# A four-layer graph network on one core: the last layer's first step sums its prepared chunks in place, and the degree count splits nodes by 800

## The chip, the cores and the metric

The kernel runs on one core of one Trainium2 chip. The metric is the device time of one execution in microseconds, lower is better. Each number of the trace comes from one profiled execution of the kernel.

## The reference

100,000 nodes with 64 features, 50,000 directed edges sorted by destination (a node has half an edge on the average). Four residual layers, each on `relu(layernorm(x))`: L0 is two graph convolutions with degree norms, L1 adds edge features, L2 is eight steps of edge attention, and L3, the last layer, is what the change is about. Cut to it:

```python
h = jnp.maximum(_layernorm(x), 0.0)
src_norm, dst_norm = deg(src) ** -0.5, deg(dst) ** -0.5     # degrees at least 1
out = w[0] * h
for step in range(10):
    m = (h * src_norm[:, None])[src]
    h = segment_sum(m, dst, 100000) * dst_norm[:, None]
    out = out + w[step + 1] * h
x = x + out
```

## The kernel before, in words

**Seats.** Every edge has a seat: 128 partitions by 392 columns (`COLS`), handled in 28 chunks of 14 columns (`CH`). Edges of one destination lie side by side in a partition, or run over into the next partition. `X[:, j, :]` holds the row of a seat's destination. After the dense part a step only works on seats: it gathers the 64 values of each seat's source, multiplies by `snE` (source norm), sums along the columns where `cont` is 1 (the same destination goes on; `sums`, L1807), multiplies by `dnorm`, adds it with weight `wk` to `X` and stores the rows as the table of the next step. Odd steps read `tab_e` and write `alt_e`, even ones the other way. A node whose source has no in-edges need not be followed further, so the seats are sorted by class, and each step gathers only the first columns: the widths `WI` are 252 columns or fewer for step two, and shrink from there.

**Step one.** It reads the rows of all 392 columns. The last ten chunks (`K3` = 10, from column `EARLY` = 252 on; 18 = `SPLIT`) have sources without in-edges, so their values come from the dense rows, and GpSimd gathers them into ten tiles ahead of the layer (`dead_rows`, L215 and L747): four in `shared`, two in `xin`, then `rowsC`, `agg`, `rowsD` (with rows 67 wide) and `spare`. If step two were wider than 252 the kernel would gather all 28 in step one (`full`, `past`, `WP`). In `step_e(1, True)` (L2258) VectorE first loops over nine pairs of gathered chunks, and then runs `last_chunk` (L2231) on the ten prepared ones in turn: it copies the rows into `G` (`copy_predicated`, L2246), multiplies, sums, multiplies with `dnorm` (L2251), and adds to `X` (L2254). The running sum `carry` passes from chunk to chunk.

**Around it.** GpSimd runs one list of work (L776): `narrow_sweep` (L660: per chunk a copy of 14 columns of indices at L672, then 14 indirect gathers at L483, buffers G[0] and G[1] in turn), ten scatters of finished rows to `out` (`early_rows`, L767), `front_sums` (L682: it waits until all stores of sums have landed, and gathers `tcar` and `FR`, the sums that cross a partition), four more scatters, `front_rows` (L691: it waits for `f_ready` and scatters `FR`), and then waits for `step_done`. ACT issues the stores of `G` (L851). VectorE turns the carried sums through PE twice (`carry_in`, L1828), signals `f_ready`, computes the next indices (`next_seats`, L2033) and waits until the early and the front rows have landed. `early_copy` (L2225) copies one chunk of `X` into `rowsA` for GpSimd's scatters, in step one after the first prepared chunk. In steps two to ten VectorE's loop has 14 turns, of which those that the width doesn't need are passed over at the start:

```python
wide_to = dve.value_load(WI[0:1, ds(k, 1)], min_val=0, max_val=COLS)
dve.reg_mov(at_pair, 0)
with dve.Fori(0, NCH // 2) as i:
    with dve.If(i * (2 * CH) + wide_to > COLS - 2 * CH):
```

After step ten VectorE signals `final_ready` (L2308), and GpSimd scatters the 252 remaining columns and the front row to `out` (L789 to L794).

**The degree count**, at the kernel's start. The number of edges of a source node is counted with products of one-hot vectors: node = `LOB` x hi + lo, with `LOB` = 1024. For each of the 392 columns VectorE compares a ramp with hi (128 columns) and with lo (1024 columns, L1321), and PE adds the products into two banks (L1099). Beside it GpSimd scatters the seats of 392 columns into `seatmap` (L522). VectorE then does the first dense tiles, and waits at L1484 until `seatmap` is read back, before it can write `lookup`.

## Time and profile before

| | before |
|---|---|
| median of 3 runs | 9275.63 us (9274.99 to 9276.62) |
| the profiled execution | 9275.27 us |
| its span | 9273.6 us |
| GpSimd, VectorE, PE busy | 6297.6, 5268.7, 1598.9 us |
| first gather of the last layer's step one | at 7219.11 us |
| first gather of its step two | at 7718.13 us |
| first of the scatters after step ten | at 8940.20 us |

The span is the time from the first to the last instruction that the profiler saw; 1.7 us of the execution lie around it. In the trace's rows PE, DVE (VectorE), ACT, POOL (GpSimd) and SP are the engines, a "q" behind one is its sequencer, which issues DMAs, and L483 is line 483 of the kernel. The indirect gathers all have the line of their helper, L483, and the scatters L487, so they are told apart by their tiles. The idle time in square brackets is that of the engine just before the instruction, with what ended it; "issue" means that the engine waited for nothing that the profile shows.

### The profile page before, as it was taken

Reading aid. Unit: us, or ns where it says so; the run is one execution under the profiler, and the core shown is the slowest. Engines: PE = TensorE matmul, PEld = TensorE weight load, DVE = VectorE, ACT = ScalarE, POOL = GpSimd, SP = SyncE. Lnnn points to the kernel's source line nnn. Section 1 sums busy time; section 2 is a strip of 40 time slices with the busy share of each in tenths; the row PEclk is TensorE's granted clock in tenths of the full one; section 3 lists DMA queues with packets and bytes.
Section 4 is the critical chain, followed back from the end, with each engine's and each line's share of the span. In section 5 each row is a group of like instructions: output and inputs, shape, how many; then the busy total and the mean of one; then the engine's idle time right before and its main releaser. Section 6 shows DMA issues by size and latency. Waiting matters only on the chain.

```text
span 9273.6 us, 59946 instructions
## 1 busy us (share of the span) xinstructions
PE 1598.9 (17%) x7434; PEld 1131.8 (12%) x7434; DVE 5268.7 (57%) x16349; ACT 581.8 (6%) x1205; POOL 6297.6 (68%) x6351
## 2 busy tenths in 40 slices
PE   5635231310355203530012200000000000000000
PEld 1124221210244202320012100000000000000000
DVE  6668464673888853446678777555548454333310
ACT  0012110100122101110000000000001000000000
POOL 6767766547777777767767577676556755677777
PEclk9855555555555555555555555555555555555555
DMA  0023111110344423333333322133322221433220
GB/s 11 4 78 108 59 61 34 66 40 0 89 134 129 120 84 82 95 82 91 91 97 113 84 46 49 42 46 42 37 30 72 48 45 41 43 42 40 35 27 19
DMA packets 604655, 568.99 MB, mean 61 GB/s; under 512 B 437740, under 2 KB 443809, under 8 KB 604496
## 3 DMA queue, kind: packets, MB, share of 16 engines
q0 software_dynamic: 189536, 151.31, 12.7%
q10 hardware_dynamic: 368192, 328.20, 10.7%
q1 hardware_dynamic: 46866, 88.94, 2.9%
q14 instruction: 56, 0.46, 0.0%
q8 instruction: 5, 0.08, 0.0%
HBM read 214.35 MB, written 357.06 MB: 62 GB/s over the span
## 4 chain that ended last, share of the span: by engine, by line
POOL 46%; issue 23%; DVE 18%; DMA 10%; POOLq 1%; DVEq 1%; PE 0%; SPq 0%; ACTq 0%; ACT 0%
POOL G L483 22%; POOL look L483 6%; DVE G L1821 5%; POOL X L483 4%; POOL pair L483 4%; POOL seatmap L487 4%; POOL out L487 3%; POOL spare L483 2%; DMA G<-tab_d,idxs 1%; DVE G L1811 1%; DMA alt_d<-G 1%; DVE xm L1370 1%; DMA G<-alt_d,idxs 1%; DVE st L1345 1%; DVE G L2103 1%
## 5 line engine op out<-in xcount | busy, mean ns | idle before, releaser
L483 POOL DMA_INDIRECT G<-tab_d,idxs x616 | 652.0, 1058 | 223.3 <-issue 178.3
L483 POOL DMA_INDIRECT look<-flagtab,idxs x588 | 613.2, 1043 | 206.7 <-issue 170.2
L483 POOL DMA_INDIRECT G<-tab_e,idxs x504 | 533.5, 1059 | 183.2 <-issue 151.9
L483 POOL DMA_INDIRECT G<-alt_e,idxs x420 | 445.0, 1060 | 157.7 <-issue 127.8
L483 POOL DMA_INDIRECT X<-in_x,dst_gat x392 | 417.0, 1064 | 154.5 <-issue 124.6
L483 POOL DMA_INDIRECT G<-tab_c,idxs x392 | 419.9, 1071 | 141.0 <-issue 111.2
L483 POOL DMA_INDIRECT G<-tab_b,idxs x392 | 419.1, 1069 | 141.1 <-issue 112.6
L483 POOL DMA_INDIRECT pair<-lookup,idxs x392 | 412.7, 1053 | 139.9 <-issue 116.1
L483 POOL DMA_INDIRECT G<-alt_d,idxs x392 | 408.8, 1043 | 141.6 <-issue 113.4
L2244 DVE TENSOR_TENSOR G<-G,chn 128x896 f32<-128x896 f32 x66 | 72.3, 1096 | 757.1 <-DMA G<-tab_e,idxs 409.2
L483 POOL DMA_INDIRECT G<-tab_a,idxs x392 | 396.7, 1012 | 142.7 <-issue 113.7
L487 POOL DMA_INDIRECT seatmap<-vals,idxs x392 | 397.7, 1015 | 140.7 <-issue 116.5
L1063 PE MATMUL TR<-w4T,shared 128*128 128x64 f32 x2356 | 464.6, 387 | 147.5 <-ACT shared L838 147.5
L1063 PEld LDWEIGHTS TR<-w4T,shared 128*128 128x128 f32 x2356 | 451.4, 298 | 241.3 <-issue 241.3
L1345 DVE BATCH_NORM_STATS2 st<-xin 128x6 f32<-128x64 f32 x3136 | 419.3, 211 | 61.4 <-DVE rowsC L1361 17.1
L1080 PE MATMUL HP<-ident,tcar 128*64 128x128 f32 (+1 forms) x21 | 8.7, 415 | 2523.6 <-DVEq L1281 2513.0
L1073 PE MATMUL TR<-w1Te,hT 64*128 64x64 f32 x1568 | 182.1, 420 | 1170.3 <-ACT hT L828 1170.3
L1821 DVE SCALAR_TENSOR_TENSOR G<-G,chn 128x64 f32<-128x64 f32 x1092 | 311.6, 285 | 39.1
L483 POOL DMA_INDIRECT G<-in_edge_attr,idxs x252 | 269.8, 1071 | 88.1 <-issue 75.3
L820 ACT ACTIVATE lnw<-lnw,lneps 128x14 f32<-128x14 f32 (+1 forms) x340 | 104.3, 307 | 3477.4 <-DVEq L1356 3454.7
L1073 PEld LDWEIGHTS TR<-w1Te,hT 64*128 64x128 f32 x1568 | 173.2, 327 | 1191.1 <-issue 1191.1
L1080 PEld LDWEIGHTS HP<-ident,tcar 128*64 128x64 f32 (+1 forms) x21 | 3.2, 151 | 2526.9 <-issue 2526.9
(491 smaller groups left out, 7515.0 us busy)
## 6 DMA issues: line engine op xcount, KB each, us to landing
raw<-G ACTq DMA_DIRECT2D x84, 448.0 KB, 3.6
tab_d<-rowsD ACTq DMA_DIRECT2D x56, 469.0 KB, 2.8
tab_d<-G ACTq DMA_DIRECT2D x56, 469.0 KB, 3.1
xin<-in_x SPq DMA_DIRECT2D x56, 448.0 KB, 5.7
tab_b<-rowsB ACTq DMA_DIRECT2D x56, 448.0 KB, 2.8
out<-shared ACTq DMA_DIRECT2D x56, 448.0 KB, 3.9
tab_c<-rowsC ACTq DMA_DIRECT2D x56, 448.0 KB, 2.5
alt_d<-G ACTq DMA_DIRECT2D x44, 469.0 KB, 2.8
```

Of the source, the lines that this page charges most:

```text
L483: pool.indirect_dma_start(to, None, table, bass.IndirectOffsetOnAxis(ap=index, axis=0), bounds_check=bound, oob_is_err=False).then_inc(s, 16)
L487: pool.indirect_dma_start(table, bass.IndirectOffsetOnAxis(ap=index, axis=0), frm, None, bounds_check=bound, oob_is_err=False).then_inc(s, 16)
L820: nc.scalar.activation(lnw[:, 4, 0:R], lnw[:, 3, 0:R], ACT.Sqrt, bias=lneps[:, 0:1], scale=1.0 / D).then_inc(sd_ready, 1)
L1063: last = nc.tensor.matmul(T[:, r * D:(r + 1) * D], U[:, r % 2, r // 2, :], w4T[:, :], start=True, stop=True)
L1073: last = nc.tensor.matmul(T[:, at:at + D], hT[h * D:(h + 1) * D, r // 2, :], w[h * D:(h + 1) * D, :], start=True, stop=True)
L1080: nc.tensor.transpose(to, frm, ident[0:n, 0:n]).then_inc(turned, 1)
L1345: last = v.bn_stats(st[:, r, :], xr[:, r, :])
L1370: v.tensor_tensor(xm[:, 0:R, :], to[:, :, 0:D], flat_rows(attn[:, k * D:(k + 1) * D], R), ALU.mult).then_inc(dve_step, 1)
L1811: v.scalar_tensor_tensor(G[:, s, j, 0:W], before, go[:, j:j + 1], G[:, s, j, 0:W], ALU.mult, ALU.add).then_inc(dve_step, 1)
L1821: v.scalar_tensor_tensor(G[:, s, j, 0:W], before, go[:, j:j + 1], G[:, s, j, 0:W], ALU.mult, ALU.add).then_inc(dve_step, 1)
L2103: v.tensor_tensor(g, g, wide(p, AW), ALU.mult).then_inc(dve_step, 1)
L2244: v.tensor_tensor(g, g, wide(chn[:, 1, :]), ALU.mult).then_inc(dve_step, 1)
```

## The change

- `dead_chunk(n)` sums a prepared chunk in its own tile, with factors `late_sn` and a running sum `late_sum` that starts at zero. `head()` replaces the loop of step one: unrolled, it runs `dead_chunk(0)`, and then nine times `last_chunk` of an even chunk, a `dead_chunk`, `last_chunk` of an odd chunk.
- Behind the last gathered chunk, `carried(n)` adds to a prepared chunk what comes over from the 18 gathered ones (`late_go`, a scan of `cont` times `dnorm`), through a tile in PSUM. Chunk 27 comes first, with its `dead_out` (the addition to `X`) and `early_copy(1)`, and then the other nine.
- SyncE stores each of these ten tiles to `alt_e`; ACT stores only the 18. GpSimd waits for `dead_stored` between the early rows and `front_sums`, in every step.
- The other nine `dead_out` stand at the end of `step_e`, which now runs for all ten steps. `base` is their weight: that of step one, and zero from then on. `early_copy(k + 1)` follows them, and takes the early rows from the last columns backwards (392 - 14k).
- Step one's turns of the loop, `turns[0]`, are 0 unless `full[:, 0]` is set, so its 14 turns are passed over.
- `past`, `past_dead` and `r_out` go.
- `LOB` is 800 and not 1024. hi and lo come from a multiplication and two corrections and not from a shift and a mask, the products have 400 columns and not 512, and hi has 125 values and not 98.

```diff
-    LOB = 1024
+    LOB = 800
...
+            for n in range(K3):
+                sp.wait_ge(dead_ready, n + 1)
+                sp.dma_start(seats(alt_e, 0, SPLIT + (n - 1) % K3), dead_rows[(n - 1) % K3]).then_inc(dead_stored, 16)
...
-            def past_dead(k):
-                for s in (0, 1):
-                    chunks = pool.value_load(past[0:1, 0, ds(k, 1)], min_val=0, max_val=NCH)
-                    pool.reg_add(r_used[s].reg, r_used[s].reg, chunks)
-                    stores = pool.value_load(past[0:1, 1, ds(k, 1)], min_val=0, max_val=16 * NCH)
-                    pool.reg_add(r_raw[s].reg, r_raw[s].reg, stores)
...
                     narrow_sweep(table, k, D, gathered3, WP)
-                    if table is tab_e:
-                        past_dead(k)
                     early_rows(0, CH - 4)
+                    pool.wait_ge(dead_stored, 16 * K3)
+                    pool.sem_inc(pool_waited, 1)
                     front_sums(to, at, last, D)
...
-                wide_to = act.value_load(WI[0:1, ds(k, 1)], min_val=0, max_val=COLS)
+                wide_to = act.value_load(WP[0:1, ds(k, 1)], min_val=0, max_val=COLS)
...
-            v.tensor_single_scalar(hi0, src0, LOB.bit_length() - 1, op=ALU.arith_shift_right)
-            v.tensor_single_scalar(lo0, src0, LOB - 1, op=ALU.bitwise_and).then_inc(dve_step, 1)
+            low, off = early(17), early(18)
+            v.tensor_scalar(hi0, src0, 1.0 / LOB, -0.48, ALU.mult, ALU.add).then_inc(dve_step, 1)
+            dve.wait_ge(dve_step, nth())
+            v.scalar_tensor_tensor(low, hi0, float(-LOB), src0, ALU.mult, ALU.add).then_inc(dve_step, 1)
+            dve.wait_ge(dve_step, nth())
+            v.tensor_scalar(off, low, 0.0, None, ALU.is_lt)
+            v.tensor_scalar(lo0, low, float(LOB), None, ALU.is_ge).then_inc(dve_step, 1)
+            dve.wait_ge(dve_step, nth())
+            v.tensor_tensor(off, lo0, off, ALU.subtract).then_inc(dve_step, 1)
+            dve.wait_ge(dve_step, nth())
+            v.tensor_tensor(hi0, hi0, off, ALU.add)
+            v.scalar_tensor_tensor(lo0, off, float(-LOB), low, ALU.mult, ALU.add).then_inc(dve_step, 1)
...
+            v.tensor_copy(turns[:, 0, 2:16], WB[0:1, 2:16])
+            v.tensor_scalar(turns[:, 0, 1:2], full[0:1, 0:1], float(COLS - EARLY), None, ALU.mult)
+            v.memset(turns[:, 1, 1:2], SPLIT // 2)
...
             def early_copy(k):
-                v.tensor_scalar(oidx[:, :], dst_out[:, ds(k * CH + (EARLY - CH), CH)], ok[:, 0:1], None, ALU.add)
-                v.tensor_copy(rowsA[:, :, :], X[:, ds(k * CH + (EARLY - CH), CH), :]).then_inc(dve_step, 1)
+                v.tensor_copy(ok[:, :], again[:, ds(k, 1)]).then_inc(dve_step, 1)
+                dve.wait_ge(dve_step, nth())
+                v.tensor_scalar(oidx[:, :], dst_out[:, ds(COLS - k * CH, CH)], ok[:, 0:1], None, ALU.add)
+                v.tensor_copy(rowsA[:, :, :], X[:, ds(COLS - k * CH, CH), :]).then_inc(dve_step, 1)
                 dve.wait_ge(dve_step, nth())
                 dve.sem_inc(early_ready, 1)
...
+            late_sn, late_go, late_sum = mx, tmpB, mrep
+
+            def dead_chunk(n):
+                r = dead_rows[n]
+                at = EARLY + n * CH
+                v.tensor_tensor(r, r, wide(late_sn[:, at:at + CH]), ALU.mult).then_inc(dve_step, 1)
+                dve.wait_ge(dve_step, nth())
+                for j in range(CH):
+                    before = late_sum[:, 0:D] if j == 0 else r[:, j - 1, :]
+                    v.scalar_tensor_tensor(r[:, j, :], before, cont[:, at + j:at + j + 1], r[:, j, :],
+                                           ALU.mult, ALU.add).then_inc(dve_step, 1)
+                    dve.wait_ge(dve_step, nth())
+                v.tensor_copy(late_sum[:, 0:D], r[:, CH - 1, :]).then_inc(dve_step, 1)
+                dve.wait_ge(dve_step, nth())
+                v.tensor_tensor(r, r, wide(dnorm[:, at:at + CH]), ALU.mult).then_inc(dve_step, 1)
+                dve.wait_ge(dve_step, nth())
+
+            def carried(n):
+                r = dead_rows[n]
+                at = EARLY + n * CH
+                t = TR_OF[n % 2][:, 0:CH * D].rearrange("p (j f) -> p j f", f=D)
+                v.tensor_tensor(t, flat_rows(late_sum[:, 0:D], CH), wide(late_go[:, at:at + CH]), ALU.mult).then_inc(dve_step, 1)
+                dve.wait_ge(dve_step, nth())
+                v.tensor_tensor(r, r, t, ALU.add).then_inc(dve_step, 1)
+                dve.wait_ge(dve_step, nth())
+                dve.sem_inc(dead_ready, 1)
+
+            def dead_out(n):
+                at = EARLY + n * CH
+                v.scalar_tensor_tensor(X[:, at:at + CH, :], dead_rows[n], base[:, 0:1], X[:, at:at + CH, :],
+                                       ALU.mult, ALU.add).then_inc(dve_step, 1)
+                dve.wait_ge(dve_step, nth())
+
+            def head():
+                v.tensor_copy(wk[:, :], mixb[:, 1:2])
+                v.tensor_scalar(late_sn[:, EARLY:COLS], snE[:, EARLY:COLS], full[:, 1:2], None, ALU.mult)
+                v.tensor_tensor_scan(late_go[:, EARLY:COLS], cont[:, EARLY:COLS], cont[:, EARLY:COLS], 1.0,
+                                     ALU.mult, ALU.mult)
+                v.memset(late_sum[:, :], 0.0)
+                v.memset(carry[:, :], 0.0).then_inc(dve_step, 1)
+                dve.wait_ge(dve_step, nth())
+                dve.wait_ge(dead_gathered, 16 * CH * K3)
+                dead_chunk(0)
+                for i in range(SPLIT // 2):
+                    fresh()
+                    last_chunk(2 * i, 0)
+                    dead_chunk(i + 1)
+                    last_chunk(2 * i + 1, 1)
+                v.tensor_tensor(late_go[:, EARLY:COLS], late_go[:, EARLY:COLS], dnorm[:, EARLY:COLS], ALU.mult)
+                v.tensor_copy(late_sum[:, 0:D], carry[:, 0:D])
+                v.tensor_copy(base[:, :], wk[:, :]).then_inc(dve_step, 1)
+                dve.wait_ge(dve_step, nth())
+                v.tensor_scalar(late_go[:, EARLY:COLS], late_go[:, EARLY:COLS], full[:, 1:2], None, ALU.mult).then_inc(dve_step, 1)
+                dve.wait_ge(dve_step, nth())
+                carried(K3 - 1)
+                dead_out(K3 - 1)
+                early_copy(1)
+                for n in range(K3 - 1):
+                    carried(n)
+
+            def step_e(k):
                 v.tensor_copy(wcol[:, :], WB[:, ds(k, 1)])
-                v.tensor_copy(ok[:, :], again[:, ds(k, 1)])
                 v.tensor_copy(wk[:, :], mixb[:, ds(k, 1)]).then_inc(dve_step, 1)
                 dve.wait_ge(dve_step, nth())
-                if not first:
-                    early_copy(k)
-                begin()
-                if first:
-                    v.tensor_copy(TR[:, 0:CH * D], full[:, 1:2].to_broadcast([P, CH * D])).then_inc(dve_step, 1)
-                    dve.wait_ge(dve_step, nth())
-                    with dve.Fori(0, SPLIT // 2) as i:
+                todo = dve.value_load(turns[0:1, 0, ds(k, 1)], min_val=0, max_val=COLS)
+                dve.reg_mov(at_pair, dve.value_load(turns[0:1, 1, ds(k, 1)], min_val=0, max_val=NCH // 2 - 1))
+                with dve.Fori(0, NCH // 2) as i:
+                    with dve.If(i * (2 * CH) + todo > COLS - 2 * CH):
                         fresh()
+                        dve.wait_ge(dead_stored, 16 * K3)
+                        pair_now = dve.snap(at_pair, min_val=0, max_val=NCH // 2 - 1)
                         for s in (0, 1):
-                            last_chunk(2 * i + s, s)
-                            r_out[s].skip(16)
-                    dve.wait_ge(dead_gathered, 16 * CH * K3)
-                    for n in range(K3):
-                        last_chunk(SPLIT + n, n % 2, dead_rows[n])
-                        if n == 0:
-                            early_copy(k)
-                    for s in (0, 1):
-                        dve.reg_mov(r_gat3[s].reg,
-                                    dve.value_load(past[0:1, 2, NCH // 2 - 1:NCH // 2], min_val=1, max_val=16 * COLS))
-                else:
-                    wide_to = dve.value_load(WI[0:1, ds(k, 1)], min_val=0, max_val=COLS)
-                    dve.reg_mov(at_pair, 0)
-                    with dve.Fori(0, NCH // 2) as i:
-                        with dve.If(i * (2 * CH) + wide_to > COLS - 2 * CH):
-                            fresh()
-                            pair_now = dve.snap(at_pair, min_val=0, max_val=NCH // 2 - 1)
-                            for s in (0, 1):
-                                last_chunk(pair_now * 2 + s, s)
-                            dve.reg_add(at_pair, at_pair, 1)
+                            last_chunk(pair_now * 2 + s, s)
+                        dve.reg_add(at_pair, at_pair, 1)
                 fresh()
                 carry_in(D)
                 v.tensor_scalar(FR[:, 0, 0:D], FR[:, 0, 0:D], dnorm[:, FC:FC + 1], None, ALU.mult).then_inc(dve_step, 1)
@@ -2298,11 +2333,15 @@
                 v.scalar_tensor_tensor(X[:, FC, :], FR[:, 0, 0:D], wk[:, 0:1], X[:, FC, :], ALU.mult, ALU.add).then_inc(dve_step, 1)
                 dve.wait_ge(dve_step, nth())
                 dve.wait_ge(early_stored, r_es.more(16 * CH))
+                for n in range(K3 - 1):
+                    dead_out(n)
+                v.memset(base[:, :], 0.0)
+                begin()
+                early_copy(k + 1)
                 dve.wait_ge(f_stored, r_fs.more(16))
 
-            step_e(1, True)
-            begin()
-            with dve.Fori(2, K3 + 1) as k:
+            head()
+            with dve.Fori(1, K3 + 1) as k:
                 fresh()
                 step_e(k)
             dve.sem_inc(final_ready, 1)
```

## Rows read from the trace of the kernel before

**Rows 1.** The page, busy time of each engine, share of the span, instructions.

```profile
PE 1598.9 (17%) x7434; PEld 1131.8 (12%) x7434; DVE 5268.7 (57%) x16349; ACT 581.8 (6%) x1205; POOL 6297.6 (68%) x6351
```

**Rows 2.** The page, the chain that ended last, share of the span by engine.

```profile
POOL 46%; issue 23%; DVE 18%; DMA 10%; POOLq 1%; DVEq 1%; PE 0%; SPq 0%; ACTq 0%; ACT 0%
```

**Rows 3.** Timeline, step one's first chunks: start, us, engine, line, what, idle before.

```profile
7219.11 1.04 POOL L483 DMA_INDIRECT G<-tab_e,idxs  x1 [1.01 <-issue]
...
7238.24 1.02 POOL L483 DMA_INDIRECT G<-tab_e,idxs  x1 [0.87 <-POOL idxs L672]
7238.71 1.09 DVE L2244 TENSOR_TENSOR G<-G,chn 128x896 f32<-128x896 f32 x1 [19.39 <-DMA G<-tab_e,idxs]
...
7245.97 1.15 DVE L2254 SCALAR_TENSOR_TENSOR X<-G,wk,X 128x896 f32 x1 [0.24 <-DVE G L2251]
...
7258.72 1.09 DVE L2244 TENSOR_TENSOR G<-G,chn 128x896 f32<-128x896 f32 x1 [10.74 <-DMA G<-tab_e,idxs]
```

**Rows 4.** Timeline, step one's end: last gathered chunk, early rows, last prepared chunk, next gather.

```profile
7580.69 1.09 DVE L2244 TENSOR_TENSOR G<-G,chn 128x896 f32<-128x896 f32 x1 [10.68 <-DMA G<-tab_e,idxs]
...
7587.88 1.15 DVE L2254 SCALAR_TENSOR_TENSOR X<-G,wk,X 128x896 f32 x1 [0.24 <-DVE G L2251]
...
7602.48 1.03 POOL L487 DMA_INDIRECT out<-rowsA,oidx  x1 [23.29 <-DVEq L2229]
...
7702.36 1.15 DVE L2254 SCALAR_TENSOR_TENSOR X<-G,wk,X 128x896 f32<-128x896 f32 x1 [0.15 <-DVE G L2251]
...
7706.88 1.05 POOL L483 DMA_INDIRECT tcar<-alt_e,fidx  x1 [90.94 <-DMA alt_e<-G]
```

**Rows 5.** Timeline, the turned sums, the start of step two and of step seven.

```profile
7710.87 0.39 PE L1080 MATMUL HP<-ident,tcar 128*64 128x128 f32 x1 [699.88 <-DVEq L1281]
...
7718.13 1.08 POOL L483 DMA_INDIRECT G<-alt_e,idxs  x1 [1.82 <-DMA alt_e<-FR,fidx]
...
7724.11 0.32 DVE L2238 COPY chn<-cont 128x14 f32 x1 [4.72 <-remote]
...
8614.94 0.17 DVE L2238 COPY chn<-cont 128x14 f32 x1 [9.23 <-remote]
```

**Rows 6.** Timeline, gathers beside VectorE's work on the first chunk.

```profile
7240.16 4.14 DVE L1811 SCALAR_TENSOR_TENSOR G<-G,chn 128x64 f32<-128x64 f32 x13
7240.99 1.00 POOL L483 DMA_INDIRECT G<-tab_e,idxs  x1 [0.30 <-issue]
...
7244.64 1.09 DVE L2251 TENSOR_TENSOR G<-G,chn 128x896 f32<-128x896 f32 x1
7244.91 1.70 POOL L483 DMA_INDIRECT G<-tab_e,idxs  x1 [0.30 <-issue]
```

**Rows 7.** DMA issues, 7200 to 8950: queue, count, size, median us to landing.

```profile
alt_e<-G ACTq DMA_DIRECT2D x46, 448.0 KB, 3.7
...
tab_e<-rowsE ACTq DMA_DIRECT2D x1, 448.0 KB, 2.4
```

**Rows 8.** Timeline, the first scatter after step ten.

```profile
8940.20 0.98 POOL L487 DMA_INDIRECT out<-X,dst_out  x1 [2.14 <-DVEq L2308]
```

**Rows 9.** Timeline of a gather beside back-to-back operations, and the gathers' min/median/max.

```profile
4160.94 1.09 DVE L1935 TENSOR_TENSOR agg<-agg,b4b 128x896 f32<-128x896 f32 x1
4161.03 1.88 POOL L483 DMA_INDIRECT G<-tab_b,idxs  x1 [0.30 <-issue]
4162.17 1.09 DVE L1937 TENSOR_TENSOR X<-X,agg 128x896 f32 x1
...
L483 POOL DMA_INDIRECT G<-tab_b,idxs x392: 1000/1004/1912, 4093.6 to 4657.5; - x196
```

**Rows 10.** Groups by line during the count (40 to 400), and VectorE's wait for seatmap.

```profile
L1321 DVE TENSOR_SCALAR X<-X,chn 128x1024 f16<-128x1024 f16 x353 | 183.4, 520 | 0.0
...
L487 POOL DMA_INDIRECT seatmap<-vals,idxs x246 | 249.7, 1015 | 88.9 <-issue 73.3 <-POOL vals L518 15.6
...
620.84 0.69 DVE L1484 COPY X<-X 98x1024 f32<-98x1024 f32 x1 [66.12 <-DMA X<-seatmap]
```

More of the change, by code:

```diff
@@ L175, in _build @@
         WP = sb("WP", [1, 16], i32)
-        past = sb("past", [1, 3, 16], i32)
+        turns = sb("turns", [1, 2, 16], i32)
         full = sb("full", [P, 2])
@@ L225, in _build @@
         MI = HP[:, 3, :]
-        HI = HP[:, 0:2, :]
+        HALF = LOB // 2
+        HI = HP[:, 0:2, 0:HALF]
         iotas = sem("iotas")
@@ L303, in _build @@
         dead_gathered = sem("dead_gathered")
+        dead_ready = sem("dead_ready")
+        dead_stored = sem("dead_stored")
         early_ready = sem("early_ready")
@@ L1904, in _ @@
             for k in range(1, K3 + 1):
-                v.memset(again[:, k:k + 1], float(EARLY + (k - 1) * CH))
+                v.memset(again[:, k:k + 1], float(COLS - k * CH if k > 1 else EARLY))
             v.memset(again[:, K3 + 1:16], float(COLS))
-            v.memset(past[:, :, :], 0)
+            v.memset(turns[:, :, :], 0)
             v.tensor_scalar(full[:, 0:1], WB[:, 2:3], float(EARLY), None, ALU.is_gt)
@@ L1912, in _ @@
             v.tensor_copy(WP[:, :], WI[:, :])
-            v.tensor_scalar(past[:, 0, 1:2], full[0:1, 1:2], float(K3 // 2), None, ALU.mult)
-            v.tensor_scalar(past[:, 1, 1:2], full[0:1, 1:2], float(16 * K3 // 2), None, ALU.mult)
-            for i in range(SPLIT // 2, NCH // 2):
-                v.tensor_scalar(past[:, 2, i:i + 1], full[0:1, 0:1], float(16 * CH * (i + 1 - SPLIT // 2)),
-                                float(16 * CH * SPLIT // 2), ALU.mult, ALU.add)
+            v.tensor_copy(turns[:, 0, 2:16], WB[0:1, 2:16])
+            v.tensor_scalar(turns[:, 0, 1:2], full[0:1, 0:1], float(COLS - EARLY), None, ALU.mult)
+            v.memset(turns[:, 1, 1:2], SPLIT // 2)
             v.tensor_tensor(again[:, 2:16], WB[:, 2:16], again[:, 2:16], ALU.is_gt)
@@ L2049, in _ @@
             at_pair = dve.alloc_register("dve_pair")
-            r_out = [Reached(dve, f"dve_out{s}", FIRST + 16 * 4 * (NCH // 2)) for s in (0, 1)]
             def step_d(k, first=False):
@@ L2241, in last_chunk @@
                 dve.wait_ge(dve_step, nth())
-                if rows is None:
-                    dve.wait_ge(gathered3[s], r_gat3[s].more(16 * CH))
-                    v.tensor_tensor(g, g, wide(chn[:, 1, :]), ALU.mult).then_inc(dve_step, 1)
-                else:
-                    v.copy_predicated(g, few, rows).then_inc(dve_step, 1)
-                    dve.wait_ge(dve_step, nth())
-                    v.tensor_tensor(g, g, wide(chn[:, 1, :]), ALU.mult).then_inc(dve_step, 1)
+                dve.wait_ge(gathered3[s], r_gat3[s].more(16 * CH))
+                v.tensor_tensor(g, g, wide(chn[:, 1, :]), ALU.mult).then_inc(dve_step, 1)
                 dve.wait_ge(dve_step, nth())
@@ L2256, in last_chunk @@
                 dve.sem_inc(used[s], 1)
-            def step_e(k, first=False):
+            late_sn, late_go, late_sum = mx, tmpB, mrep
[13 more added lines that the diff above has]
+                dve.wait_ge(dve_step, nth())
```

19 lines of the change are left out of this document (5 added, 14 removed).

## The prediction

> **What bounds the kernel now.** I read the page first: GpSimd is busy 68% of the span and VectorE 57% [rows 1], and the chain that ended last lies on GpSimd for 46% and on "issue" for 23% [rows 2], the 0.30 us between two indirect DMAs. So a change pays where it shortens GpSimd's sequence or a time in which GpSimd waits.
>
> Then the timeline of the last layer's step one. GpSimd gathers 18 chunks of 14 from 7219.11 on; the first one's sums start on VectorE at 7238.71 and the eighteenth's at 7580.69 [rows 3, 4], so 20.1 us a chunk. VectorE has a chunk done in 8.4 us (7238.71 to 7247.12) and idles 10.74 us before the next one [rows 3]. After the last gather the picture turns round: VectorE takes the ten prepared chunks in turn, from 7589.0 to 7703.5, 11.45 us each. GpSimd has only ten scatters of early rows from 7602.48 on, and then idles 90.94 us, until the last store of sums has landed and `tcar` can be gathered at 7706.88 [rows 4]. This is what the change is after. In all later steps GpSimd gathers without such a gap, and after step ten its 252 scatters begin 2.14 us after the last row [rows 8].
>
> **Step one, removed and put in its place.** From the start of the last gathered chunk's sums (7580.69) to `tcar` (7706.88) it is 126.2 us [rows 4]. After the change:
> - the same chunk's own sums: 8.3 us, as now;
> - three small preparations (two over 128x140): 0.7 us, between 0.2 and 1.5; no row has them;
> - `carried` for chunk 27: two operations of 896 columns, 1.09 us each like L2251 [rows 6] and 0.04 us between, 2.3 us;
> - its `dead_out`, the form of L2254: 1.15 us [rows 3], 1.2 with its wait; `early_copy`: three short operations, 1.2 us. GpSimd so gets its early rows about 7600, plus the delays below, much as now;
> - nine more `carried`, 9 x 2.26 = 20.3 us;
> - SyncE's last store and `tcar` behind it. Stores of this size land in 3.7 us from G, 2.4 from a dense tile [rows 7]; now 4.4 us pass from the last sums' store (with L2254 at 7702.4) to `tcar` [rows 4]. Chunk 26 lies in rowsD, strided like G, so I keep it: 4.5 us. At 2.26 us a piece the stores can overlap; were they served one after another at 3.7, the last would land 9 us later.
> Sum 38.6 us, a gain of **87.6**.
>
> What it costs there: the ten `dead_chunk` take 1.13 + 14 x 0.32 + 0.23 + 1.13 = 7.0 us each (14 sums at the pace of the 13 in 4.14 us [rows 6], L1814 for the copy). Nine fall into the idle 10.7 us after every even chunk, the first before any data is there: the cover holds with 3 us to spare, and if it failed, VectorE would still have another idle stretch one chunk on. But they are not free for GpSimd. An indirect DMA that starts while VectorE runs a long operation on two SBUF inputs waits for it: 1.70 us instead of 1.00 beside L2251, while beside the short sums it stays 1.00 [rows 6]. The first chunk, with no such work beside it, took 19.13 us to the next one's first gather (7238.24), the mean is 20.1 [rows 3, 4]: 0.97 for three long operations, with a hiccup or two, so 0.3 each. Twenty more make **+6** (bounds 0, and 20 x 0.97). GpSimd's first copy of indices meets the first one: +0.8.
>
> After `carried`, VectorE still passes the 14 empty turns of step one's loop. It idles 4.72 us before the first chunk of a step that passes over 5 turns and 9.23 with 13 [rows 5], so 0.56 a turn and 1.9 for a load; now 14 turns and two loads, 0.5 + 3.8 + 7.9 = 12.2 us after about 7620.7. The turned sums are wanted 4.0 us after `tcar` (7710.87 [rows 5]). VectorE is 3.4 us late; GpSimd's four remaining scatters cover about 1.5: **+1.9** (0 to 3.4). Step one in all: **-78.9**.
>
> **All ten steps: the nine `dead_out`.** They stand in `step_e`, so each step does them (with factor 0 after the first): 9 x 1.19 = 10.7 us of VectorE, begun when the early rows have landed, in step one about 2 us before the next gather of 7718.13 [rows 5]. In nine steps GpSimd starts gathering at the same time (7718.13), so VectorE itself is covered: up to the first chunk's data there are some 20 us, which the train, `early_copy`, the loads and up to 13 empty turns just fill; a few us late on a first chunk is made good before the second, since VectorE needs 8.4 of 20. But the long operations stand back to back beside the gathers. How that goes L1933 to L1937 show: the gather started in L1935 took 1.88, got in at its end, and the next started 0.3 us behind it [rows 9]. Two gathers in three operations would be +0.95 each 3.5 us; over 9.4 us I take 2.2 a step, 9 x 2.2 = **+20** (0; or each gather stretched, 4.0 a step, +36). After step ten nothing covers it: GpSimd waits for `final_ready`, 2.14 us now [rows 8]. The train 10.7 and `early_copy`(11) 1.3, less 1 because the early rows land before the front row: **+11.1** (10 to 13). The waits on `dead_stored` after the first are long fulfilled: under 0.1 us each. `past_dead`, four loads behind each odd step's last gather, is removed at nothing: GpSimd ran it ahead and is in any case waiting for the last store there.
>
> **LOB 800.** The count's 392 comparisons of 1024 columns become shorter (0.52 us now, at most 22% less), as do PE's products. It saves no path: beside it GpSimd's 392 scatters into seatmap run on, and VectorE idles 66.12 us before L1484 for them [rows 10]; it will idle longer. What remains is that these scatters take 1015 ns in the mean [rows 10], where an undisturbed one of the same line takes 0.98 [rows 8]: 246 x 0.035 = 8 us of stretching, of which shorter operations give back perhaps 2.5 (bounds: gain 8; loss 3 for tables of another size in HBM). The six added operations of the division by 800 lie before the count, hidden by the same wait. **-2.5**.
>
> The ACT loop takes its width from WP: it issues 18 stores for step one instead of 28, off the path.
>
> **The sum**: -78.9 + 20 + 11.1 - 2.5 = -50.3. The profiled execution took 9275.27 us (span 9273.6, 1.7 around it) and the median of the three is 9275.63; 9275.27 - 50.3 gives **9225**.
>
> **Rivals.** One, the lock-out: no indirect DMA gets in between back-to-back long operations of VectorE, since they leave only 0.04 us, so GpSimd stands still for each whole train, 9.4 us from 7718.1: 9 x 9.4 = 85 instead of 20, and every one of the twenty in step one costs 0.97 instead of 0.3, 13.4 more. -50.3 + 65 + 13.4 = +28, 9303, slower than before. It decides from 7.8 us a step end on. Against it: the 1.88 us gather got in after one operation, and no gather into G from tab_b lasted over 1.91 [rows 9]. For it: no train of nine is in this trace.
> Two, trains free: the long operations at a step's end happen not to meet the gathers, or need no common port. 9225 - 20 - 6 = 9199. Against it are the 1.70 and 1.88. The Trainium skill, "SBUF — State Buffer", section "Who interferes with whom", says that a VectorE instruction with two SBUF inputs contends with GpSimd's reads, and infers that descriptor generation wants only the write interface. The 1.70 us [rows 6] agrees with the first and speaks against the inference; by the inference the trains would be free and the time this rival's.
> Three, the stores in a row: SyncE's ten stores go one after another at 3.7 us and compete with ten scatters; the last lands 9.5 us later, which hides the late VectorE: +7.6, 9233. For it: stores from G are all of short rows; against it: dense tiles took 2.4.
> Four, the change does not engage, if step one's width is over 252: the first and the last gathered chunk's sums lie 342 us apart, which is 17 chunks, with ten prepared ones behind them [rows 3, 4], so no.
>
> **Chances.** Forecast 0.75 (own range 9206 to 9245), rival one 0.05, two 0.07, three 0.10, others 0.03. The range 9199 to 9256 takes in two and three, and the trains at their dear end (+16) with the dearer stretches of step one (+13). What a measurement of this kernel tells from no change is about 0.2%, 19 us: faster means below 9257, reached by all but rival one and dear ends together: 0.89; within 0.07; slower 0.04.
>
> **What would show it.** `tcar` of step one starts at about 7626 instead of 7706.88 (7706.88 - 87.6 + 6 + 0.8); GpSimd idles only a few us before it, on the store. The 18 chunks last about 367 us. The first chunk of steps two to ten takes about 2.2 us longer, with one or two gathers of 1.9 us. The last scatters begin about 13 us after the last front row. If the chunk times of step one grow by over 1 us each, or if the first chunks grow by over 4, I am wrong on the port; if `tcar` comes after 7640, on the stores or on the cover.

## The result, and the profile after

The changed kernel takes 9226.5 us (median of 4 runs, 9224.5 to 9230.9), the kernel before beside it 9275.3: the ratio is 0.9949, with a 95% interval of 0.9937 to 0.9961. The forecast was 9225, with a range of 9199 to 9256. The total is right to 2 us; of its terms one had the wrong sign. The profiled execution took 9230.85 us, its span is 9229.1.

Its page, the span and the busy times, and the chain that ended last:

```profile
span 9229.1 us, 59901 instructions
...
PE 1616.4 (18%) x7434; PEld 1163.3 (13%) x7434; DVE 5359.7 (58%) x16431; ACT 582.1 (6%) x1205; POOL 6338.6 (69%) x6351
...
POOL 45%; issue 23%; DVE 20%; DMA 9%; POOLq 1%; DVEq 1%; PE 0%; SPq 0%; ACTq 0%; ACT 0%
```

VectorE is busy for 91 us more than in [rows 1] and GpSimd for 41 us more, and yet the kernel is faster. VectorE's work was added where it had been waiting. GpSimd executes the same 6351 instructions, so its 41 us are no work but instructions that last longer: 23.5 us of it in the last layer's gathers into `G`, 10.0 in the gathers from `tab_d`, which the change doesn't touch.

The timeline of step one's end, which answers to [rows 4]. In the changed kernel the gathers have line L489, the scatters L493:

```profile
7592.48 1.09 DVE L2243 TENSOR_TENSOR G<-G,chn 128x896 f32<-128x896 f32 x1 [4.60 <-DMA G<-tab_e,idxs]
...
7601.70 1.10 DVE L2274 TENSOR_TENSOR TR<-mrep,tmpB 128x896 f32<-128x896 f32 x1
7602.84 1.09 DVE L2276 TENSOR_TENSOR spare<-spare,TR 128x896 f32<-128x896 f32 x1
...
7607.19 1.17 POOL L493 DMA_INDIRECT out<-rowsA,oidx  x1 [16.18 <-DVEq L2234]
...
7626.44 1.09 DVE L2276 TENSOR_TENSOR rowsD<-rowsD,TR 128x896 f32<-128x896 f32 x1
7627.61 0.38 SPq L466 DMA_DIRECT2D alt_e<-rowsD  x1
...
7632.22 1.05 POOL L489 DMA_INDIRECT tcar<-alt_e,fidx  x1 [9.71 <-issue]
...
7639.31 0.39 PE L1079 MATMUL HP<-ident,tcar 128*64 128x128 f32 x1 [620.94 <-DVEq L1280]
...
7645.77 1.07 POOL L489 DMA_INDIRECT G<-alt_e,idxs  x1 [1.02 <-issue]
```

From the last gathered chunk's sums to `tcar` it is now 39.7 us (7592.48 to 7632.22) where it was 126.2; the last store goes out at 7627.61, has landed 3.5 us later, and `tcar` starts 4.6 us behind it. GpSimd's wait of 90.94 us in [rows 4] has become one of 9.71.

The start of step three, where the nine `dead_out` stand (L2282, a "train" of nine operations), beside the gathers, and `early_copy` behind them (L2232); and the first scatter after step ten, where [rows 8] had 2.14 us:

```profile
8047.05 4.73 DVE L2282 SCALAR_TENSOR_TENSOR X<-shared,base,X 128x896 f32<-128x896 f32 x4 [1.00 <-DMA out<-rowsA,oidx]
...
8051.81 2.34 DVE L2282 SCALAR_TENSOR_TENSOR X<-xin,base,X 128x896 f32<-128x896 f32 x2
8051.97 1.86 POOL L489 DMA_INDIRECT G<-tab_e,idxs  x1 [0.30 <-issue]
8054.14 1.00 POOL L489 DMA_INDIRECT G<-tab_e,idxs  x1 [0.30 <-issue]
...
8056.61 1.15 DVE L2282 SCALAR_TENSOR_TENSOR X<-rowsD,base,X 128x896 f32<-128x896 f32 x1
8056.76 1.88 POOL L489 DMA_INDIRECT G<-tab_e,idxs  x1 [0.30 <-issue]
...
8058.74 0.62 DVE L2232 COPY rowsA<-X 128x896 f32 x1
8058.94 1.30 POOL L489 DMA_INDIRECT G<-tab_e,idxs  x1 [0.30 <-issue]
...
8895.56 0.98 POOL L493 DMA_INDIRECT out<-X,dst_out  x1 [13.39 <-DVEq L2347]
```

Two gathers beside the train are held up (1.86 and 1.88 us), the others last 1.00 to 1.07. Which of the gathers that meet such an operation are held isn't shown.

The seat map's end, which answers to the last row of [rows 10]:

```profile
614.88 0.97 POOL L493 DMA_INDIRECT seatmap<-vals,idxs  x1 [0.30 <-issue]
617.07 0.29 SPq L404 DMA_DIRECT2D X<-seatmap  x1
622.19 0.58 DVE L1493 COPY X<-X 125x800 f32<-125x800 f32 x1 [79.75 <-DMA X<-seatmap]
...
632.89 1.07 POOL L489 DMA_INDIRECT pair<-lookup,idxs  x1 [0.90 <-POOL idxs L538]
```

VectorE idles 79.75 us here instead of 66.12, as forecast. But from the last scatter to the first gather of pairs it is 18.0 us, where it was 12.4. That was not forecast.

To compare kernels I cut each profiled execution at instructions that all have. A: start of the last scatter into `seatmap` to the first gather of pairs. B: from there to step one's first gather; the kernels differ in it only in small operations of VectorE (`turns` for `past`), and at its end by the first `dead_chunk`, beside which GpSimd's copy of indices takes 0.62 us and not 0.19. C: to step two's first gather. D: to the last front row's scatter. E: to the first scatter behind `final_ready`.

| kernel | A | B | C | D | E |
|---|---|---|---|---|---|
| before | 12.4 | 6591.3 | 499.0 | 1219.0 | 3.1 |
| after | 18.0 | 6593.0 | 419.9 | 1235.4 | 14.4 |
| after, once more | 18.5 | 6592.1 | 421.3 | 1234.7 | 14.4 |
| after, LOB 1024 | 12.5 | 6581.2 | 420.5 | 1232.7 | 14.4 |
| before, LOB 800 | 18.2 | 6584.8 | 498.7 | 1215.2 | 3.1 |
| after, LOB 784 | 10.8 | 6588.7 | 420.8 | 1234.1 | 14.4 |
| after, LOB 896 | 12.1 | 6588.1 | 420.8 | 1234.9 | 14.4 |
| after, dead_out once | 18.3 | 6585.8 | 420.9 | 1213.9 | 4.0 |
| after, trains in PSUM | 18.1 | 6579.3 | 420.9 | 1218.1 | 15.2 |
| after, nine dead_chunk left out | 18.2 | 6586.4 | 417.2 | 1236.1 | 14.4 |
| after, no empty turns | 18.3 | 6586.0 | 418.3 | 1233.2 | 14.4 |
| PSUM chunks | 18.1 | 6590.8 | 415.6 | 1187.0 | 4.0 |
| combined | 11.0 | 6575.7 | 401.6 | 1185.3 | 4.0 |

Two readings. Between before and after A, B, C, D and E give +5.6, +1.7, -79.1, +16.4 and +11.3, which with -0.5 ahead of A is, to 0.1, the difference of the spans, -44.5. And B, in which hardly anything was edited, moves between 6575.7 and 6593.0, so medians get several microseconds there that can't be put down to an edit. A, C, D and E repeat to 2 us (after and after once more), D of the kernels before to 4. That B moves by chance is inferred: the two executions of the changed kernel are 0.9 us apart in it, but five executions of that kernel range from 9220.8 to 9235.4 us, and the other stretches leave no room for that. The kernel before, run beside the others, had medians of 9275.3, 9269.6, 9272.8 and 9272.9 us, so kernels that were run at different times are better compared by their ratios to it than by their medians.

### The profile page after: what moved, and what is told of

Its sections match the earlier page's. It is cut to its first block, busy times and chain, and to the rows that moved or that the text cites. A ratio compares the mean times of both kernels' runs of the same rounds, so it can differ in the third digit from the quotient of the medians.

```text
span 9229.1 us, 59901 instructions
## 1 busy us (share of the span) xinstructions
PE 1616.4 (18%) x7434; PEld 1163.3 (13%) x7434; DVE 5359.7 (58%) x16431; ACT 582.1 (6%) x1205; POOL 6338.6 (69%) x6351
## 4 chain that ended last, share of the span: by engine, by line
POOL 45%; issue 23%; DVE 20%; DMA 9%; POOLq 1%; DVEq 1%; PE 0%; SPq 0%; ACTq 0%; ACT 0%
POOL G L489 21%; DVE G L1830 6%; POOL look L489 6%; POOL X L489 4%; POOL pair L489 4%; POOL seatmap L493 4%; POOL out L493 3%; POOL spare L489 2%; DVE st L1354 1%; DMA G<-tab_d,idxs 1%; DMA alt_d<-G 1%; DVE xm L1379 1%; DMA G<-alt_d,idxs 1%; DVE G L2109 1%; DVE G L1382 1%
## 5 line engine op out<-in xcount | busy, mean ns | idle before, releaser
L489 POOL DMA_INDIRECT G<-tab_d,idxs x616 | 662.0, 1075 | 223.4 <-issue 182.7
L489 POOL DMA_INDIRECT look<-flagtab,idxs x588 | 612.4, 1042 | 206.7 <-issue 170.2
L489 POOL DMA_INDIRECT G<-tab_e,idxs x504 | 547.2, 1086 | 182.4 <-issue 154.7
L489 POOL DMA_INDIRECT G<-alt_e,idxs x420 | 454.8, 1083 | 156.9 <-issue 132.7
L489 POOL DMA_INDIRECT X<-in_x,dst_gat x392 | 414.4, 1057 | 149.5 <-issue 124.3
L489 POOL DMA_INDIRECT G<-tab_c,idxs x392 | 419.9, 1071 | 141.0 <-issue 111.8
L489 POOL DMA_INDIRECT G<-tab_b,idxs x392 | 416.5, 1062 | 141.1 <-issue 110.1
L489 POOL DMA_INDIRECT pair<-lookup,idxs x392 | 413.2, 1054 | 139.9 <-issue 116.1
L489 POOL DMA_INDIRECT G<-alt_d,idxs x392 | 408.2, 1041 | 141.8 <-issue 115.2
L493 POOL DMA_INDIRECT seatmap<-vals,idxs x392 | 401.4, 1024 | 140.9 <-issue 116.6
L489 POOL DMA_INDIRECT G<-tab_a,idxs x392 | 396.6, 1012 | 142.7 <-issue 112.8
L489 POOL DMA_INDIRECT G<-in_edge_attr,idxs x252 | 271.3, 1076 | 89.3 <-issue 75.2
```

The costliest lines, as they stand in the source:

```text
L489: pool.indirect_dma_start(to, None, table, bass.IndirectOffsetOnAxis(ap=index, axis=0), bounds_check=bound, oob_is_err=False).then_inc(s, 16)
L493: pool.indirect_dma_start(table, bass.IndirectOffsetOnAxis(ap=index, axis=0), frm, None, bounds_check=bound, oob_is_err=False).then_inc(s, 16)
```

## Experiments

### The count: LOB

```diff
-    LOB = 800
+    LOB = 1024
```

> The changed kernel with LOB 1024 again (the count alone is undone). Theory A, from the changed kernel's profile: LOB 800 lost time, since the map's load and the lookup's store of 125 rows run at a third of the DMA engines' share that 98 rows had. Then the load is back in 3.3 us, the first pair gather again starts about 10.4 us behind the last seating scatter's end instead of 15.9, and the time is 5 to 6 us under the changed kernel, about 9221. Rival B, as predicted: the shorter comparisons gave GpSimd time back, and this one is 2.5 us slower, about 9229. What separates them is a fixed pair of transfers, so the trace decides even if the medians don't.

A is 12.5 us, 5.5 less than in the changed kernel: theory A. (The 15.9 of the expectation is the wait up to the copy of indices ahead of the first gather; to the gather itself it was 17.0 us from the last scatter's end.) The median is 9214.4 us, 12 to 15 less than the changed kernel's two medians, but its ratio to the kernel before is 0.9942 (0.9928 to 0.9956) against 0.9949 and 0.9952, which is 6 to 9 us and within the intervals. B was 11 us short in the profiled one, and so nothing beyond A is put down to LOB.

The other way round, the kernel before with LOB 800, two banks of 400 columns and the division by 800:

> The kernel before with the count of LOB 800 alone. Theory A (the two transfers of 125 rows are slower): first pair gather 5 us later behind the last seating scatter, time 9280 to 9281, 5 us over the kernel before. Rival B (comparisons): 2.5 us under it, 9272.5.

A is 18.2 again, 5.7 us more than with 1024. The median is 9270.8 against 9269.6 of before, ratio 1.0 with an interval of 0.9991 to 1.0009, so 8 us either way. Beside 9269.6 the theory would have been about 9275 and the rival about 9267, so the median decides nothing, and A is the theory's: the time of a stretch of 12 us can be read from a trace, not from medians that B moves by several microseconds. As to the shorter comparisons: first to last start of the scatters into `seatmap` is 574.2 and 577.0 us with 1024, and between 573.0 and 579.8 in eight executions with 800. No gain can be seen.

Why is A longer? The DMA view from 616 to 634 us of the changed kernel, and from 619 to 631 of the one with LOB 1024: busy tenths of the 16 DMA engines in 40 slices, the queue's packets, MB and share, and the load of `xin` that stands behind the lookup's store:

```profile
DMA  0000403323321000133879733324331222310000
...
q1 hardware_dynamic: 404, 1.66, 27.0%
...
xin<-in_x SPq DMA_DIRECT2D x1, 448.0 KB, 9.1
```

```profile
DMA  0000000947873000000099799789986779410000
...
q1 hardware_dynamic: 368, 1.66, 44.6%
```

The first group of digits is the load of the map: mostly 2 or 3 tenths with 125 rows, mostly 7 or more with 98. In the second group the lookup's store of 125 rows begins at 3 tenths and runs on at 2 to 4 when `xin` has been loaded beside it. Two sizes tell the number of rows from their length:

```diff
-    LOB = 800
+    LOB = 784    # and 896 in the next run
```

> The changed kernel with LOB 784: the map's load and the lookup's store then have 128 rows of 3136 and 6272 bytes. The profile shows the DMA engines 0.3 busy with 125 rows (5 of 16 is 0.31) and 0.8 with 98 (14 of 16 is 0.88): as if a transfer used as many engines as the largest divisor of its rows up to 16. Theory A, that divisor: 128 rows take 16 engines, so the first pair gather comes 12 to 12.5 us behind the start of the last seating scatter, as with 98 rows, though the rows are the shortest of all. Rival B, short rows: 784 is then no better than 800, 18 us or more.

> The changed kernel with LOB 896: 112 rows of 3584 and 7168 bytes. Theory A, the divisor (16 engines): first pair gather 12 to 12.5 us behind the start of the last seating scatter. Rival B, the length of a row: between 12.5 (1024) and 18 (800), about 15.

A is 10.8 us with 128 rows, the shortest rows of all, and 12.1 with 112; the rival falls with both. The two single executions took 9218.2 and 9222.0 us. LOB 784, from 615 to 625 us:

```profile
DMA  0000000098779710000000899999990978994100
...
q1 hardware_dynamic: 432, 1.66, 49.1%
...
xin<-in_x SPq DMA_DIRECT2D x1, 448.0 KB, 4.4
```

The Trainium skill, "DMA: Bandwidth & Descriptors", section "Why a DMA increments its semaphore by 16 and not by 1", says that a transfer is spread over the largest number of engines up to 16 that divides the slowest dimension on both of its sides. By that rule 98, 125, 112 and 128 rows take 14, 5, 16 and 16 engines, and the order of the four measured A (12.4, 18.0, 12.1, 10.8) agrees. What makes 112 rows 1.3 us slower than 128, with 16 engines each by the rule, isn't shown: the lookup's store landed in 4.5 and 3.5 us, `xin` in 5.2 and 4.4.

### The trains of dead_out

```diff
                 dve.wait_ge(early_stored, r_es.more(16 * CH))
-                for n in range(K3 - 1):
-                    dead_out(n)
-                v.memset(base[:, :], 0.0)
                 begin()
+                with dve.If(k < 2):
+                    for n in range(K3 - 1):
+                        dead_out(n)
+                fresh()
```

> The changed kernel, with the nine dead_out done in step one only (in the nine later steps they add the rows with factor 0, so nothing is left out). If the trains cost GpSimd 2 us a step beside its gathers and 11.25 us uncovered after step ten, as I forecast: 8 trains x 2.0 and 10.7 of the end, 26 to 27 us less than the changed kernel, about 9199 to 9200; gathers of 1.9 us at a step's start are gone in steps two to nine. Rival: the trains beside gathers cost nothing and the 16.5 us that steps two to ten lost came from elsewhere (the early copy that now stands at the step's end, the other order of waits): then only 10.7 less, about 9216.

9198.9 us, ratio to the kernel before 0.9923 (0.9910 to 0.9937), with 9199 to 9200 expected. E falls from 14.4 to 4.0. D falls to 1213.9; in the six executions that have all trains and differ from the changed kernel in LOB or the turns alone, its mean is 1234.2, so 20.3 us more. But not all of that are trains. They stand beside the first chunk of a step, and from its first gather to the next chunk's it is 21.2 us in the changed kernel, 19.2 in this one and in the kernel before: 2.1 for a train with the `early_copy` behind it, 17 us for eight (two gathers held by 0.87 each, one by 0.30). The other 3 to 4 us lie elsewhere in D and are of the size by which D varies without an edit. The theory holds, and its 2.0 a step too. The start of step three has no long gather left:

```profile
8046.69 0.11 DVE L1813 MEMSET carry<- 128x67 f32 x1 [1.04 <-DMA out<-rowsA,oidx]
...
8048.72 1.07 POOL L489 DMA_INDIRECT G<-tab_e,idxs  x1 [1.50 <-DMA tab_e<-FR,fidx]
...
8051.41 1.00 POOL L489 DMA_INDIRECT G<-tab_e,idxs  x1 [0.31 <-issue]
8052.72 1.00 POOL L489 DMA_INDIRECT G<-tab_e,idxs  x1 [0.30 <-issue]
```

Is it VectorE's work as such, or the second operand in SBUF? On top of this edit, the same trains in steps two to ten, with the second operand and the output in PSUM (the code is cut):

```diff
+                with dve.If(k > 1):
+                    for n in range(K3 - 1):
+                        v.scalar_tensor_tensor(TR_OF[n % 2][:, 0:CH * D]..., dead_rows[n], base[:, 0:1],
+                                               TR_OF[(n + 1) % 2][:, 0:CH * D]..., ALU.mult, ALU.add)
```

> The changed kernel, with the nine dead_out in step one only, and in steps two to ten in their place nine operations of the same form and length that have one operand in SBUF, one in PSUM and their output in PSUM (a scratch; nothing is left out). VectorE is as busy as in the changed kernel, and the end after step ten is uncovered as there. If it is the second SBUF operand that shuts out the gathers' descriptors: no gather of over 1.5 us in the trains, the first chunks 1.8 us shorter, 16 us less than the changed kernel, about 9210. If any back-to-back work of VectorE delays a gather: as the changed kernel, 9226.

9210.4 us, as the theory of the second operand has it (E is 15.2, uncovered as before). A first chunk takes 19.5 us: 0.3 more than without the train instead of 2.1, and the 0.3 are the one gather that meets `early_copy` (1.32 us). D is 1218.1, 4 us over the kernel without the later trains, again within what D varies by. VectorE is as busy, and the gathers beside the train aren't slowed:

```profile
8038.83 4.73 DVE L2343 SCALAR_TENSOR_TENSOR TR<-shared,base,TR 128x896 f32<-128x896 f32 x4 [0.42 <-DVE carry L1813]
...
8044.32 1.00 POOL L489 DMA_INDIRECT G<-tab_e,idxs  x1 [0.30 <-issue]
...
8045.98 1.16 DVE L2343 SCALAR_TENSOR_TENSOR TR<-rowsC,base,TR 128x896 f32<-128x896 f32 x1
8046.94 1.00 POOL L489 DMA_INDIRECT G<-tab_e,idxs  x1 [0.30 <-issue]
```

This run moves the second operand and the output at once, so by itself it could be the output as well; the chunks of the kernels further below, whose products write to SBUF with their second operand in PSUM and leave the gathers at 1.00 and 1.01 us, say that it is the operand.

The section that the prediction took its rule from (the Trainium skill, "SBUF — State Buffer", "Who interferes with whom") also says that a VectorE instruction with at most one SBUF input and outside the two-port modes does not contend with GpSimd; the gathers of 1.00 us here agree. Its inference on descriptor generation does not agree with the 1.86 and 1.88 us of the changed kernel: an operation with two SBUF inputs holds an indirect DMA up.

### The cost of dead_chunk in step one

```diff
                     last_chunk(2 * i, 0)
-                    dead_chunk(i + 1)
                     last_chunk(2 * i + 1, 1)
```

> The changed kernel without nine of the ten dead_chunk (the sums of nine prepared chunks are left out, so their part of the result is). It measures what they cost GpSimd's 18 chunks beside them. By my forecast 0.3 us for each long operation, 18 operations, 5 to 5.5 us: first to last gather's end of step one 360 us instead of 365.1. Rival: they cost nothing and the 5 us are from the start (the first copy of indices) or from elsewhere: 364 to 365.

First to last gather's start of step one is 359.0 us (7226.0 to 7585.0) instead of 364.1 (7225.9 to 7590.0), 5.1 less. The changed kernel's is the lowest of the eight executions that have these operations and the old chunks, which give 364.1 to 365.5 and 364.8 in the mean: so 5.8 us for 18 long operations, 0.32 each. A chunk that has a `dead_chunk` beside it takes 20.7 us in the changed kernel and 20.0 here, the others 19.8 in both. The single execution took 9228.9 us, which says nothing about an edit of 5 us. In C only 2.7 us of the 5.1 arrive, as VectorE idles 13.90 us ahead of the turned sums instead of 11.49, passing the same 14 empty turns; why that took longer isn't shown.

### The empty turns

```diff
+                with dve.If(todo > 0):
-                with dve.Fori(0, NCH // 2) as i:
+                    with dve.Fori(0, NCH // 2) as i:
```

> The changed kernel with a branch around the loop of step one when it has no turn to do. If it is the 14 empty turns and the loads that make VectorE late for the turned front sums after tcar (idle 11.49 us until something not on record, 7.1 us from tcar to the first of these operations where 4.0 were enough before), the first operation comes 4.0 us after tcar and step two's first gather 11.3 to 11.6 instead of 13.55: -2 us in all. Rival: it waits for TensorE, whose own part starts from the same front rows, and nothing changes.

The rows that answer to the last three of the first timeline:

```profile
7630.07 1.05 POOL L489 DMA_INDIRECT tcar<-alt_e,fidx  x1 [9.71 <-issue]
...
7634.08 0.39 PE L1079 MATMUL HP<-ident,tcar 128*64 128x128 f32 x1 [619.52 <-DVEq L1280]
...
7641.48 1.07 POOL L489 DMA_INDIRECT G<-alt_e,idxs  x1 [1.02 <-issue]
```

PE starts 4.0 us after `tcar` instead of 7.1, the next step 11.4 us after it instead of 13.55, as expected. The single execution took 9224.5 us, which by itself shows nothing.

### No second SBUF operand in a chunk

If a second operand in SBUF is what costs, every gathered chunk pays too, the kernel before included ([rows 6]: 1.70). So, on top of `dead_out` in step one only (waits left out, and the short copies that put the factors into PSUM):

```diff
-                v.tensor_tensor(g, g, wide(chn[:, 1, :]), ALU.mult)
+                v.tensor_tensor(g, g, wide(pc[:, 0, :]), ALU.mult)      # pc, pg: in PSUM
                 sums(s, D, chn[:, 0, :])
-                v.tensor_tensor(g, g, wide(chn[:, 2, :]), ALU.mult)
+                v.tensor_tensor(g, g, wide(pc[:, 1, :]), ALU.mult)
                 dve.sem_inc(raw_ready, 1)
-                v.scalar_tensor_tensor(xcols(c), g, wk[:, 0:1], xcols(c), ALU.mult, ALU.add)
+                v.tensor_copy(pg, g)
+                v.scalar_tensor_tensor(xcols(c), pg, wk[:, 0:1], xcols(c), ALU.mult, ALU.add)
```

> The kernel with nine dead_out in step one only, and each gathered chunk of the last layer changed so that none of its long operations reads two operands from SBUF: the factors of the two products lie in PSUM, and the sums are copied to PSUM (one more operation of 896 columns) before they are added to X. Theory, the shared port: a chunk's two late operations now cost GpSimd 0.97 us (20.1 us a chunk against 19.13 without them), which goes: 66 chunks x 0.97 = 64 us, 9135. The copy to PSUM doesn't stall, no more than the nine of 9.4 us to PSUM did, where the gathers beside them took 1.00. VectorE has 8.4 + 1.1 us of work in 19.1, so it stays covered. Rival: the 0.97 are stalls behind any work, or short operations take them over: 9195 to 9200 as now.

9167.5 us, ratio 0.9887 (0.9870 to 0.9903): 31 us under the kernel it builds on, half of what I expected. The mechanism holds, the size didn't. GpSimd's groups of the last layer (7230 us to the end), busy and mean ns, first of the kernel with `dead_out` once, then of this one:

```profile
L489 POOL DMA_INDIRECT G<-alt_e,idxs x420 | 445.2, 1060 | 157.7 <-issue 129.4 <-POOL idxs L678 21.8 <-DMA alt_e<-FR,fidx 6.2
...
L489 POOL DMA_INDIRECT tcar<-tab_e,fidx x5 | 5.2, 1049 | 20.9 <-DMA tab_e<-G 20.9
```

```profile
L489 POOL DMA_INDIRECT G<-alt_e,idxs x420 | 425.4, 1013 | 153.8 <-issue 123.8 <-POOL idxs L678 21.8 <-DMA alt_e<-FR,fidx 7.3
...
L489 POOL DMA_INDIRECT tcar<-tab_e,fidx x5 | 5.3, 1050 | 26.4 <-DMA tab_e<-G 26.4
```

A gather takes 1013 ns in the mean instead of 1060. The estimate of 64 us was wrong in three ways. The ten first chunks of a step have nothing beside them: 39 chunks of steps two to ten and 17 of step one are left, not 66. The 39 became 31 us shorter, 0.8 each and not 0.97, and the 17 only 6.3 us together, as `dead_chunk` with its two SBUF operands still stands beside half of them (0.7 a chunk without it, 0.3 with it). And about 5 us went back between the steps: the wait for the last store ahead of `tcar` grew from 20.9 to 26.4 us over five steps, since VectorE's last chunk and its store are the path when the gathers end sooner.

### All together

The same for the two products of `dead_chunk` (factors copied to PSUM), LOB 784, and the branch around the empty turns:

> What the runs point to, together: dead_out in step one only, no second SBUF operand in a gathered chunk's long operations (as in the run before), the same for the factors of dead_chunk, LOB 784, and the 14 empty turns of step one passed in one branch. From the run with the PSUM chunks (9167.5): LOB 784 -6 (first pair gather 624.6 - 613.9 = 10.7 us behind the last seating scatter against 18.0), dead_chunk -9 (the chunks beside one take 20.3 us there, the others 19.25, nine times), empty turns -2 to -3: about 9150. If the dead_chunk's stretch isn't the port, 9159.

9140.3 us (median of 4 runs, 9125.7 to 9144.5) where about 9150 were expected, ratio to the kernel before 0.9859 (0.9844 to 0.9874): 1.4% faster than it, and 86 to 89 us faster than the changed kernel's medians. Step one's chunks follow each other every 19.1 to 19.4 us but for two of 21.0, which every kernel has, with `dead_chunk` beside them or not. The longest of its 252 gathers takes 1061 ns (1698 in the changed kernel), though these products write to SBUF:

```profile
7267.55 1.09 DVE L2266 TENSOR_TENSOR shared<-shared,TR 128x896 f32<-128x896 f32 x1
7267.67 1.00 POOL L489 DMA_INDIRECT G<-tab_e,idxs  x1 [0.30 <-issue]
...
7273.42 1.09 DVE L2275 TENSOR_TENSOR shared<-shared,TR 128x896 f32<-128x896 f32 x1
7274.21 1.00 POOL L489 DMA_INDIRECT G<-tab_e,idxs  x1 [0.30 <-issue]
```

C is 14.0 us less than with the PSUM chunks alone (11.4 of it in step one's gathers, about 2.1 from the turns), A 7.1, D 1.7; the remaining 4.4 of the median's 27.2 are of the size by which B varies.

### The changed kernel once more

> The changed kernel itself once more, beside the others on the same chip, to compare them with. The first profiled execution spent 1705.3 us between the first gather from tab_d and the first prepared gather, where the four variants that leave that part alone spent 1690.6 to 1696.5. If that was chance, it comes out near 9222 here and in that band; if it belongs to the change, at 1705 again.

9229.2 us, ratio 0.9952 (0.9939 to 0.9966), as the first time, and not the 9222 of chance alone. The stretch in question took 1699.2 us, above the band and under 1705; in the kernel before it was 1698.5. So the 1705.3 can't be put down to the change, and what moves the stretch wasn't tried.

## Why the prediction was right, and where not

**Step one** (forecast -78.9, measured -79.1 in C). The path was as described, and three small errors cancelled. The tail of 38.6 us took 39.7, so the gain is 86.5 and not 87.6: a `carried` comes every 2.37 us instead of 2.26, and `tcar` starts 4.6 us behind the last store instead of 4.5, with none of the queueing of rival three. The stretch of the 18 chunks was given as +6 and +0.8 and is 5.0 (364.1 us against 359.1), 5.8 in the mean of eight executions, with 0.32 for a long operation where the prediction took 0.3. The late VectorE was given as +1.9 and is 2.3, 2.1 of it taken back by the branch. It was late by 3.1 us (7.1 against 4.0), where the prediction wrote 3.4, though its own times give 2.8; the four scatters covered 0.8 of it and not 1.5. `tcar` was forecast at 7626 and started at 7632.22, but step one had itself started 6.8 us later (A, and what B varies by).

**Nine trains** (forecast +20, from 2.2 a step). The nine first chunks took 191.0 us instead of 173.0, +18.0, or 2.0 a step: 1.86, 1.88 and 1.30 (beside `early_copy`) in step three, where the prediction had only a single 1.88 us gather to go by [rows 9] and didn't count `early_copy`. D as a whole grew by 16.4; the rest of D is 1.6 less, within the 4 us by which the kernels before differ (1219.0 and 1215.2). Rival one, the lock-out, fell: the gather of 8051.97 meets an operation that ends 1.0 us later and lasts 0.86 us longer than others, so it didn't wait for the next operation (1.19 us more) as well. Rival two, trains free, fell with the kernel that has them once only.

**After step ten** (forecast +11.1): +11.3.

**LOB 800** (forecast -2.5, bounds -8 and +3): +5.6 in A, outside its own bounds. This is the step that failed. It was read as VectorE's comparisons, and these changed nothing that can be seen; "tables of another size in HBM" was named as the possible loss and bounded at 3, with no row of a transfer with such a number of rows. The two transfers that follow the count weren't looked at: their shape changed with LOB, and nothing hides them. What the runs showed in place of the forecast: the map's load took 5.1 us with 125 rows where it took 3.3 with 98, the whole stretch 18.0 instead of 12.4, and with 128 rows 10.8.

**The sum.** -79.1 + 16.4 + 11.3 + 5.6 is -45.8, against -50.3; the medians say -48.8, since the profiled execution is 4 us over its median. The terms' errors, 8 us on LOB and -4 on D, stand against each other, and B adds a few microseconds that belong to no term: that the total came within 2 us is luck. That it was within 10 is not, as step one, the largest term by far, was right in its path.

## What to carry to other kernels

Where GpSimd's indirect DMAs set the pace, count VectorE's operations by their SBUF inputs: a long one (896 columns) with two holds a gather up by as much as 0.9 us, and each such operation cost 0.2 to 0.3 us in the mean; one with its second operand in PSUM left the gathers at 1.00; short ones of 64 columns with two did too [rows 6]. An extra copy to PSUM was well spent as VectorE had slack. Work that adds zero is not free where it ends a step: take it out of the loop. And before a transfer's shape is changed, look at the divisors of its number of rows.

## What was not expected of the hardware

125 rows of 3200 bytes load in 5.1 to 5.6 us (issue to the copy that waits for them), 98 of 4096 in 3.3, 128 of 3136 in 3.1 and 3.2, for about the same 390 KB. A train of 10.7 us on VectorE with only one operand in SBUF left the gathers beside it at 1.00 and 1.01 us, but for the step's first (1.07, and as long without a train). And a copy from SBUF to SBUF of 896 columns that takes only 0.62 us holds a gather up by about 0.3 (1.30 us beside `early_copy` in step three, 1.28 to 1.38 in all kernels where a gather meets it behind the train), though it has only one input.
